# Heads finished in the projection, split float32r products and wide softmax tiles in a decoder layer

## The chip, the cores and the metric

The kernel runs on one NeuronCore of a Trainium2 chip. The metric is the device time of the whole kernel in microseconds. Engines are named as in the profile: PE is TensorE, DVE is VectorE, ACT is ScalarE, POOL is GpSimd, SP is SyncE, which issues the DMAs. Each runs its own instructions in their order, and they wait for each other through semaphores.

## The reference, cut to what matters

x holds 16 sequences of 128 tokens and 1024 features, in float32. One decoder layer: self-attention over the 128 tokens, cross-attention of a linear kind to a context of the same shape, and a gated feed-forward network with 4-bit weights (untouched by the change).

```
h = layernorm(x)
q, k, v = split(clip(h @ Wqkv.T, -8, 8))           # 1024 columns each
q = layernorm(q) * q_w + q_b;  k = layernorm(k) * k_w + k_b
scores = q @ k.T * 32**-0.5 + slope[head] * (j - i)  # 32 heads of 32, causal
x = x + softmax(scores) @ v @ Wout.T
# cross-attention: the 128 tokens are the channels, the 1024 features the positions
q2 = softmax(Wq @ layernorm(x), over the 64 of a head) * 64**-0.5   # 8 heads of 64
k2 = softmax(Wk @ ctx, over the 1024 positions);  v2 = Wv @ ctx
y = Wo @ ((k2 @ v2.T).T @ q2) + bo           # per head
x = x + y / norm(y, over 128 channels) * g * sqrt(128)
x = x + ffn(layernorm(x))
```

## The kernel before

It has three stages, one after another.

**Projection** (`qkv_phase`, L155). The 16 row tiles are normalised, transposed on PE and kept as a high and a low float32r part (`xT_hi`, `xT_lo`). The 3072 output columns come in six chunks of 512. For each chunk the weights are loaded in eight pieces through two staging slots, split by ACT (high, L231) and DVE (low, L255), and for each of the 16 tiles PE runs one product of 24 float32r matmuls: three terms (high x high, high x low, low x high) for each of eight blocks of the contraction (`product`, L309). DVE clips the result (L282), SP stores it to the tensor `qkv`.

**Attention** (`attention_phase`, L316). One turn for each of the 16 sequences, plus one. Turn b does the self-attention of sequence b ("own") and the cross-attention's query side of sequence b-1 ("cross"); it prepares sequence b+1 ("ahead"). Each engine has a function for its part of a turn (`turn_tensor` L510, `turn_scalar` L646, `turn_gpsimd` L691, `turn_vector` L730, `turn_sync` L490); the order in it is written out by hand. The body has 12 steps. In step t PE makes the scores of four heads (a tile of 128 x 512, L527), transposes the probabilities of tile t-2 (L519), multiplies tile t-3 by v (L548), makes a query tile of the cross-attention (L537), and in turns a key tile (L558), its transposes (L564), and their product with the context (L575). DVE adds the bias and takes maxima (L481, L487); ACT takes four exponentials of 128 columns with the maximum as bias and the sum as side result (L656); POOL multiplies by the reciprocal (L697).

After the steps PE multiplies for y (L604), projects by `Wout` in two halves of 24 matmuls, and between them transposes the next sequence's normalised q and k (`transpose_qk`, L421) and sums the squares of y (L626). After the second half come the context transposes (L438) and a product with a diagonal matrix that spreads 1/norm over the partitions (L643). The layer norm of q and k runs here: DVE takes statistics of `qk_in` (`qk_statistics`), POOL normalises (`normalise_qk`), ACT applies weight and bias from the transposed tiles (`norm_qk_affine`, L431) and DVE spreads k into the block-diagonal `kD` (`key_blocks`, L475). Query, key, score and norm products are float32.

**Feed-forward** (`feed_forward_phase`).

## Time and profile before

| | us |
|---|---|
| median of 3 runs | 3303.28 (3303.07 to 3303.88) |
| span of the profiled execution | 3299.9 |
| PE busy | 3128.8 |
| DVE busy | 1773.3 |
| ACT busy | 1045.8 |
| POOL busy | 507.1 |

The profile is of one execution. Its span runs from the first instruction to the last; the rest of that execution's own time is not in the records, and the median of the runs is 3.4 us above the span. Busy times are sums over an engine's instructions. Ends of matmuls are modelled: a row "x8" lasts longer than eight starts are apart, since the last one's own time is in it.

### The profile page before, as it was taken

The numbers are of one execution on the slowest core, as the hardware profiler recorded it, in microseconds if no ns is written. First come the engines' busy times: TensorE is split into PE (matmuls) and PEld (weight loads), VectorE is DVE, ScalarE is ACT, GpSimd is POOL, SyncE is SP. The second block draws the span as 40 slices with busy tenths as digits, with TensorE's granted clock in tenths as the row PEclk, the third lists the DMA queues.
The fourth block names the chain that finished last, engine by engine and source line by source line (L and its number), as shares of the span: only waits on it lengthen the run. The fifth ranks groups of instructions, "written<-read, shape, count | busy, mean of one in ns | idle before, by whom it ended". The sixth has DMA issues, their size and how long they took to land. (4 is left out here: it accounts for less than half of the span.)

```text
span 3299.9 us, 41826 instructions
## 1 busy us (share of the span) xinstructions
PE 3128.8 (95%) x15136; PEld 2393.9 (73%) x15136; DVE 1773.3 (54%) x2927; ACT 1045.8 (32%) x2356; POOL 507.1 (15%) x525
## 2 busy tenths in 40 slices
PE   7999997799999999999996799999999899999998
PEld 6888886566666666666663688888887788888887
DVE  5311112466666666666663655555555655555555
ACT  2100000566665566666651211111111211111111
POOL 2100000233333333333332100000000100000000
PEclk9999999899999999999996899999999999999999
DMA  4222223111111111111110432222122521231222
GB/s 144 93 73 75 73 70 116 41 39 38 43 46 51 38 38 39 50 38 51 38 33 31 129 82 55 76 65 75 54 82 76 153 64 54 81 81 54 62 74 78
DMA packets 83350, 218.73 MB, mean 66 GB/s; under 512 B 11984, under 2 KB 18256, under 8 KB 81232
## 3 DMA queue, kind: packets, MB, share of 16 engines
q1 hardware_dynamic: 83280, 217.78, 21.8%
q8 instruction: 46, 0.75, 0.1%
q14 instruction: 24, 0.20, 0.0%
HBM read 175.79 MB, written 41.94 MB: 66 GB/s over the span
## 5 line engine op out<-in xcount | busy, mean ns | idle before, releaser
L312 PE MATMUL ff_ps<-h_xT_hi,w_hi 128*128 128x512 f32 x1376 | 538.2, 391 | 13.2 <-DVE h_xT_lo L96 13.2
L312 PE MATMUL ff_ps<-h_xT_lo,w_hi 128*128 128x512 f32 x1376 | 537.1, 390 | 0.0
L312 PE MATMUL ff_ps<-h_xT_hi,w_lo 128*128 128x512 f32 x1376 | 537.0, 390 | 0.0
L1042 ACT ACTIVATE w_hi<-words 128x1024 fp32r<-128x1024 f32 x134 | 142.5, 1063 | 697.3 <-DVE words L1087 697.3
L1127 DVE TENSOR_TENSOR acc<-ff_po,acc 128x512 f32<-128x512 f32 x352 | 243.0, 692 | 210.6 <-PE ff_po L312 209.9
L312 PE MATMUL qkv_acc<-w_hi,xT_hi 128*128 128x512 f32 x768 | 300.9, 392 | 9.2 <-DVE w_lo L255 9.2
L312 PEld LDWEIGHTS ff_ps<-h_xT_hi,w_hi 128*128 128x128 f32 x1376 | 259.5, 189 | 68.3 <-issue 8.8
L312 PE MATMUL qkv_acc<-w_hi,xT_lo 128*128 128x512 f32 x768 | 299.4, 390 | 0.0
L312 PE MATMUL qkv_acc<-w_lo,xT_hi 128*128 128x512 f32 x768 | 299.3, 390 | 0.0
L312 PEld LDWEIGHTS ff_ps<-h_xT_hi,w_lo 128*128 128x128 f32 x1376 | 259.4, 189 | 54.1
L312 PEld LDWEIGHTS ff_ps<-h_xT_lo,w_hi 128*128 128x128 f32 x1376 | 259.6, 189 | 53.8
L312 PE MATMUL ff_po<-w_hi,h_hi 128*128 128x512 f32 x704 | 276.3, 393 | 10.1 <-DVE h_lo L1119 10.1
L282 DVE TENSOR_SCALAR qkv_out<-qkv_acc 128x512 f32<-128x512 f32 x96 | 66.4, 692 | 395.1 <-PE qkv_acc L312 395.1
L312 PE MATMUL ff_po<-w_lo,h_hi 128*128 128x512 f32 x704 | 275.8, 392 | 0.0
L312 PE MATMUL ff_po<-w_hi,h_lo 128*128 128x512 f32 x704 | 275.6, 391 | 0.0
L1115 DVE TENSOR_TENSOR gate<-gate,ff_ps 128x512 f32<-128x512 f32 (+1 forms) x88 | 60.3, 686 | 345.4 <-PE ff_ps L312 344.7
L656 ACT ACTIVATE scores<-scores,neg_max 128x128 f32<-128x128 f32 x512 | 199.2, 390 | 120.0 <-DVE neg_max L487 120.0
L231 ACT ACTIVATE w_hi<-w_stage 128x512 fp32r<-128x512 f32 x56 | 35.4, 632 | 452.8 <-DMA w_stage<-in_w_attn 452.8
L697 POOL TENSOR_TENSOR scores<-scores,row_rec 128x512 f32<-128x512 f32 x128 | 133.2, 1041 | 293.3 <-DVE row_rec L765 293.3
L312 PEld LDWEIGHTS qkv_acc<-w_hi,xT_hi 128*128 128x128 f32 x768 | 144.6, 188 | 39.1 <-DVE w_lo L255 9.6
L1087 DVE TENSOR_TENSOR words<-words,sc 128x1024 f32<-128x1024 int32 x134 | 164.2, 1226 | 4.6
L312 PEld LDWEIGHTS qkv_acc<-w_hi,xT_lo 128*128 128x128 f32 x768 | 144.4, 188 | 30.2
(156 smaller groups left out, 5305.9 us busy)
## 6 DMA issues: line engine op xcount, KB each, us to landing
words<-in_w SPq DMA_DIRECT2D x90, 512.0 KB, 3.5
qkv<-qkv_out SPq DMA_DIRECT2D x96, 256.0 KB, 2.0
words<-in_w SPq DMA_DIRECT2D x176, 128.0 KB, 4.0
sc<-in_s SPq DMA_DIRECT2D x88, 256.0 KB, 4.3
qk_in<-qkv SPq DMA_DIRECT2D x16, 1024.0 KB, 4.9
w_stage<-in_w_attn SPq DMA_DIRECT2D x56, 256.0 KB, 3.0
qkv_rows<-in_x SPq DMA_DIRECT2D x16, 512.0 KB, 3.8
ctx_in<-in_context SPq DMA_DIRECT2D x16, 512.0 KB, 3.7
```

What stands on the lines that cost most here:

```text
L231: nc.scalar.activation(dst[:, r, :], stage[:, r % 2, :], ACT.Copy).then_inc(w_hi_done, 1)
L282: nc.vector.tensor_scalar(res[:, :], acc[:, t % BANKS, :], CLIP, -CLIP, ALU.min, ALU.max).then_inc(clipped, 1)
L312: last = nc.tensor.matmul(out, left, right, start=n == 0, stop=n == len(pairs) - 1)
L656: last = nc.scalar.activation(sc[:, t % SR, j, :], sc[:, t % SR, j, :], ACT.Exp, bias=neg_max[:, t, j:j + 1], accum_out=row_sum[:, t, j:j ...
L697: nc.gpsimd.tensor_tensor(sc[:, n % SR, :, :], sc[:, n % SR, :, :], row_rec[:, n, :].unsqueeze(2).to_broadcast([P, HG, P]), ALU.mult).then ...
L1042: nc.scalar.activation(dst, src, ACT.Copy).then_inc(s["split_hi"], 1)
L1087: nc.vector.tensor_tensor(dst, src, scale, ALU.mult).then_inc(s["scaled"], 1)
L1115: nc.vector.tensor_tensor(gate[sl][0:units, :], gate[sl][0:units, :], b, ALU.mult).then_inc(s["product"], 1)
L1127: nc.vector.tensor_tensor(cols, po[:, o % 4, :], cols, ALU.add).then_inc(s["added"], 1)
```

## The change

In the projection (now `projection_phase`) the row tiles are taken in two halves of eight, so there are 12 rounds (two halves of six chunks), all written out without a loop. Clipped q and k stay on chip until both chunks of a row tile are there; then DVE has their statistics, POOL normalises, PE transposes and ACT applies weight and bias; SP stores them transposed as `qh` and `kh`. v is clipped and stored as before, through two slots. The first weights go to a buffer of their own. Rows 8 to 15 are loaded and normalised in the sixth round (`ci == 5`).

In attention, q comes as it is used, and k is loaded straight into the diagonal blocks of `kD` by four DMAs. The query and key products of the cross-attention become three-term float32r products (`wqk_hi`, `wqk_lo`, `xn_hi`, `xn_lo`, `ctx_hi`, `ctx_lo`). Score tiles 1, 3, 5 and 7 are "wide": POOL subtracts the maxima, ACT takes one exponential of 512 columns, DVE sums. The body has 10 steps: what steps 0 and 1 did (scores 0 and 1, key tile 0, the first transposes) now stands at the end of the turn before (`second_lead`, `lead_scalar`). 1/norm is spread by eight transposes of a broadcast column. kT holds two tiles; y has a tile of its own.

```diff
+    TILES = NB // 2
+    ROUNDS = 2 * QKV_CHUNKS
...
+    def follows(ci, t, tiles):
+
+        was = ci * TILES + t - tiles
+        if was < 0 or was // TILES % QKV_CHUNKS not in (1, 3):
+            return None
+        return heads_before(was // TILES, was % TILES)
...
+            for r in range(0, KT, 2):
+                if r == 2:
+                    load_rows(1)
+                sp.dma_start(left[:, r:r + 2, :], w_attn[0, :, r:r + 2, :]).then_inc(w_first[r // 2], 16)
...
+            for ci in range(ROUNDS):
+                half, chunk = half_and_chunk(ci)
+                for t in range(TILES):
+                    load(ci + 1, t)
+                    if ci == 0 and t + 3 < TILES:
                         load_rows(t + 3)
-                    if t % 2 == 0:
-                        load(c + 1, t // 2)
-                    sp.wait_ge(clipped, c * NB + t + 1 + BANKS)
-                    sp.dma_start(qkv[t, :, bass.ds(c * N, N)], res[:, :]).then_inc(stored, 16)
-
-            chunks(sp, chunk)
-            sp.wait_ge(stored, 16 * (QKV_CHUNKS * NB + 1))
+                    if ci == 4 and t < 2:
+                        load_rows(TILES + t)
+                    if (m := follows(ci, t, 2)) is not None:
+                        store_heads(m)
+                    if chunk >= 4:
+                        n = values_before(ci, t)
+                        sp.wait_ge(s["clipped"], ci * TILES + t + 1)
+                        sp.dma_start(v[half * TILES + t, :, (chunk - 4) * N:(chunk - 3) * N],
+                                     res[:, n % 2, :]).then_inc(v_stored[n % 2], 16)
+                    if ci == 5 and t + 2 < TILES:
+                        load_rows(TILES + t + 2)
...
+            def normalise_heads(m):
+                t, p = m % TILES, m % 2
+                pool.wait_ge(s["h_mom"], m + 1)
+                nc.gpsimd.tensor_tensor(h_mom[:, p, 4:5], h_mom[:, p, 3:4], half_neg[:, :], ALU.pow).then_inc(
+                    s["h_rstd"], 1)
+                pool.wait_ge(s["h_rstd"], m + 1)
+                for part in (left[:, t, :], right[:, p, :]):
+                    last = nc.gpsimd.tensor_scalar(part, part, h_mom[:, p, 2:3], h_mom[:, p, 4:5], ALU.add, ALU.mult)
+                last.then_inc(s["h_normed"], 1)
...
+            def scale_heads(m):
+                kind = m // TILES % 2
+                if m == 0:
+                    act.wait_ge(s["affine_in"], 4 * 16)
+                act.wait_ge(s["h_turned"], m + 1)
+                if m >= 2:
+                    act.wait_ge(h_stored[m % 2], m // 2 * 16)
+                for k in range(KT):
+                    last = nc.scalar.activation(heads[:, m % 2, k, :], room[m % 2][:, k, :], ACT.Identity,
+                                                scale=affine[:, 2 * kind, k:k + 1],
+                                                bias=affine[:, 2 * kind + 1, k:k + 1])
+                last.then_inc(s["h_out"], 1)
...
+                nc.vector.tensor_scalar(dst, acc[:, at % 4, :], CLIP, -CLIP, ALU.min, ALU.max).then_inc(
+                    s["clipped"], 1)
+                if chunk < 4:
+                    dve.wait_ge(s["clipped"], at + 1)
+                    first = chunk % 2 * 6
+                    nc.vector.bn_stats(h_stats[:, t, first:first + 6], dst).then_inc(s["h_stats"], 1)
...
+                    if ci == 5:
+                        if t == 0:
+                            statistics(TILES)
+                        if t + 1 < TILES:
+                            statistics(TILES + t + 1)
...
+                    low(ci + 1, t, w_hi[1 - ci % 2], w_lo[1 - ci % 2])
+                    clip(ci, t)
+                    if ci % QKV_CHUNKS in (1, 3):
+                        head_moments(ci, t)
+                    if ci == 5:
+                        ln.low(dve, TILES + t, t, room[t % 2])
...
+            def turn_heads(m):
+                pe.wait_ge(s["h_normed"], m + 1)
+                if m >= 2:
+                    pe.wait_ge(s["h_out"], m - 1)
+                for k in range(KT):
+                    part_of = (left[:, m % TILES, :], right[:, m % 2, :])[k // 4]
+                    last = nc.tensor.transpose(room[m % 2][:, k, :], part_of[:, k % 4 * P:(k % 4 + 1) * P], ident[:, :])
+                last.then_inc(s["h_turned"], 1)
...
+                    part(ci, t)
+                    if (m := follows(ci, t, 1)) is not None:
+                        turn_heads(m)
+                    if ci == 5:
+                        if t == 0:
+                            pe.wait_ge(s["h_out"], 2 * TILES)
+                        ln.transpose(pe, TILES + t, t % 2, room[t % 2])
...
+    WIDE = (1, 3, 5, 7)
...
+    def load_heads(sp, b):
+        sp.dma_start(hT[:, :, :], qh[b, :, :].rearrange("p (a d) -> p a d", a=KT)).then_inc(s["q_loaded"], 16)
+        for j in range(HG):
+            at = slice(j * HD, (j + 1) * HD)
+            sp.dma_start(kD[at, :, j, :], kh[b, at, :].rearrange("p (a d) -> p a d", a=KT)).then_inc(s["kd_loaded"], 16)
...
+    def keys(pe, b, i):
+        for e in range(2):
+            at = slice(e * N, (e + 1) * N)
+            last = product(nc, pair_k[:, at], [(w[:, 1, i * P:(i + 1) * P], c[:, at]) for w, c in (
+                (wqk_hi, ctx_hi), (wqk_hi, ctx_lo), (wqk_lo, ctx_hi))])
+        last.then_inc(s["k_done"], 1)
...
+    def exponentials(act, b, t):
+        if t in WIDE:
+            act.wait_ge(s["s_subbed"], wide_count(b, t))
+            last = nc.scalar.activation(sc[:, t % SR, :, :], sc[:, t % SR, :, :], ACT.Exp)
+        else:
+            act.wait_ge(s["s_max"], b * G + t + 1)
+            for j in range(HG):
+                last = nc.scalar.activation(sc[:, t % SR, j, :], sc[:, t % SR, j, :], ACT.Exp,
+                                            bias=neg_max[:, t, j:j + 1], accum_out=row_sum[:, t, j:j + 1])
+        last.then_inc(s["s_exp"], 1)
...
+    def keys_out(act, b, i):
+        act.wait_ge(s["kt_done"], b * XT + i + 1)
+        if i >= 2:
+            act.wait_ge(s["m_done"], b * XT + i - 1)
+        nc.scalar.activation(flat(kT[:, i % 2, :, :]), pair_k[:, :], ACT.Copy).then_inc(s["kt_out"], 1)
...
+    def rows_high(act, c, e):
+        act.wait_ge(s["x1_norm"], 2 * c + e + 1)
+        at = slice(e * N, (e + 1) * N)
+        nc.scalar.activation(xn_hi[:, at], xn[:, at], ACT.Copy).then_inc(s["xn_hi_done"], 1)
+
+    def rows_low(dve, c, e):
+        dve.wait_ge(s["xn_hi_done"], 2 * c + e + 1)
+        at = slice(e * N, (e + 1) * N)
+        nc.vector.tensor_tensor(xn_lo[:, at], xn[:, at], xn_hi[:, at].bitcast(F32), ALU.subtract).then_inc(
...
+    def subtract_maxima(pool, b, t):
+        pool.wait_ge(s["s_max"], b * G + t + 1)
+        nc.gpsimd.tensor_tensor(sc[:, t % SR, :, :], sc[:, t % SR, :, :],
+                                neg_max[:, t, :].unsqueeze(2).to_broadcast([P, HG, P]), ALU.add).then_inc(
+            s["s_subbed"], 1)
+
+    def reciprocals(dve, b, t):
+        dve.wait_ge(s["s_exp"], b * G + t + 1)
+        if t in WIDE:
+            nc.vector.tensor_reduce(row_sum[:, t, :], sc[:, t % SR, :, :], AX.X, ALU.add).then_inc(s["s_summed"], 1)
+            dve.wait_ge(s["s_summed"], wide_count(b, t))
+        nc.vector.reciprocal(row_rec[:, t, :], row_sum[:, t, :]).then_inc(s["s_rec"], 1)
...
+        if ahead:
+            sp.wait_ge(s["ctx_lo_done"], b + 1)
+            sp.wait_ge(s["c_done"], b + 1)
+            sp.dma_start(ctx_in[:, :], ctx_kv[b + 1, :, :]).then_inc(s["ctx_loaded"], 16)
...
+            sp.wait_ge(s["s_done"], (b + 1) * G)
+            load_heads(sp, b + 1)
             sp.wait_ge(s["o_done"], b + 1)
+            sp.dma_start(v_in[:, :], v[b + 1, :, :]).then_inc(s["v_loaded"], 16)
...
+                at = slice(j * P, (j + 1) * P)
+                product(nc, bank_q[:, :], [(r[:, at], w[:, 0, :]) for r, w in (
+                    (xn_hi, wqk_hi), (xn_hi, wqk_lo), (xn_lo, wqk_hi))]).then_inc(s["q_done"], 1)
...
+            scores(pe, b + 1, 0)
...
+            pe.wait_ge(s["ctx_lo_done"], b + 2)
+            keys(pe, b + 1, 0)
...
+            for k in range(KT):
+                last = nc.tensor.transpose(norm_banks[k // 4][:, k % 4, :],
+                                           n_sq[:, 1, k:k + 1].to_broadcast([P, P]), ident[:, :])
...
+    def second_lead(pe, b):
+        pe.wait_ge(s["s_biased"], b * G + 1)
+        scores(pe, b, 1)
+        turn_probabilities(pe, b, 0)
+        turn_keys(pe, b, 0)
+        pe.wait_ge(s["kt_out"], b * XT + 1)
+        transpose_context(pe, b)
...
+    def lead_scalar(act, b, follows=True):
+        exponentials(act, b, 0)
+        key_exponentials(act, b, 0)
+        exponentials(act, b, 1)
+        probabilities_out(act, b, 0)
+        keys_out(act, b, 0)
+        if follows:
+            rows_high(act, b - 1, 0)
+        context_out(act, b)
+        if follows:
+            rows_high(act, b - 1, 1)
...
+        for j in range(STEPS):
+            n = j + 1
+            if own and n < G:
+                normalise_scores(pool, b, n)
+            if own and j + 2 in WIDE:
+                subtract_maxima(pool, b, j + 2)
...
+        if ahead:
+            subtract_maxima(pool, b + 1, 1)
...
+            if own and j + 2 < G:
+                bias_scores(dve, b, j + 2)
+            if own and j + 1 in WIDE[1:]:
+                reciprocals(dve, b, j + 1)
...
+                context_low(dve, b + 1)
...
+        if ahead:
+            bias_scores(dve, b + 1, 0)
+            maxima(dve, b + 1, 0)
...
+            reciprocals(dve, b + 1, 0)
...
+        if ahead:
+            key_maxima(dve, b + 1, 0)
...
+            bias_scores(dve, b + 1, 1)
+            maxima(dve, b + 1, 1)
+        if own:
+            rows_low(dve, b, 0)
+        if ahead:
+            reciprocals(dve, b + 1, 1)
+        if own:
+            rows_low(dve, b, 1)
```

## Rows read from the trace of the kernel before

**Rows 1.** The page, parts 1: span; busy time (share of the span) and instructions of the TensorE.

```profile
span 3299.9 us, 41826 instructions
...
PE 3128.8 (95%) x15136; PEld 2393.9 (73%) x15136; DVE 1773.3 (54%) x2927; ACT 1045.8 (32%) x2356; POOL 507.1 (15%) x525
```

**Rows 2.** Instructions on `qkv_acc`: count, ns min/median/max, first and last start.

```profile
L312 PE MATMUL qkv_acc<-w_hi,xT_hi x768: 389/389/796, 24.1 to 559.9; 128*128 128x512 f32 x192
```

**Rows 3.** PE timeline, turns 0 and 1: start, us, line, tiles, count, [idle before].

```profile
636.64 0.50 PE L312 MATMUL pair_o<-w_hi,oT_hi 128*128 128x512 f32 x1
...
664.99 1.02 PE L537 MATMUL bank_q<-wqk_sb,xn 128*128 128x512 f32 x2
...
673.50 1.02 PE L527 MATMUL bank_s<-kD,qkT 128*128 128x512 f32 x2
...
684.12 1.02 PE L527 MATMUL bank_s<-kD,qkT 128*128 128x512 f32 x2
...
705.11 3.60 PE L604 MATMUL bank_s<-qT,z 128*128 128x512 f32 x8
```

**Rows 4.** PE timeline, the last two turns of attention.

```profile
1725.57 3.60 PE L604 MATMUL bank_s<-qT,z 128*128 128x512 f32 x8
...
1759.10 2.07 PE L537 MATMUL bank_q<-wqk_sb,xn 128*128 128x512 f32 x2 [0.66 <-DVE qr L752]
```

**Rows 5.** PE timeline, one steady turn.

```profile
1012.27 0.40 PE L312 MATMUL pair_o<-w_lo,oT_hi 128*128 128x512 f32 x1
...
1017.64 1.03 PE L438 MATMUL pair_k<-ident,ctx_in 128*128 128x128 f32 x8
1018.52 1.02 PE L643 MATMUL bank_q<-xn,ones 128*128 128x512 f32 x2
...
1021.09 1.88 PE L558 MATMUL pair_k<-ctx_in,wqk_sb 128*128 128x512 f32 x4
...
1025.94 1.09 PE L564 MATMUL pair_k<-ident,kE 128*128 128x128 f32 x8 [2.11 <-ACT kE L673]
...
1027.37 1.92 PE L527 MATMUL bank_s<-kD,qkT 128*128 128x512 f32 x2
```

**Rows 6.** One stretch of attention: us; busy (x count) of PE, PEld, DVE, ACT, POOL; PEclk; DMA.

```profile
1001.00:1075.00 74.00, 70.99 (x397) 46.65 (x396) 48.69 (x100) 45.44 (x122) 27.24 (x28) 0.98 0.14 43
```

**Rows 7.** All engines in order of time, the start of the kernel.

```profile
11.65 1.20 POOL L79 TENSOR_SCALAR qkv_rows<-qkv_rows,ln_moments 128x1024 f32<-128x1024 f32 x1
12.27 1.11 DVE L255 TENSOR_TENSOR w_lo<-w_stage,w_hi 128x512 fp32r<-128x512 f32 x1 [1.13 <-ACT w_hi L231]
...
24.07 0.80 PE L312 MATMUL qkv_acc<-w_hi,xT_hi 128*128 128x512 f32 x1 [9.20 <-DVE w_lo L255]
```

**Rows 8.** The page, part 6: DMA issues, count, KB each, us to landing.

```profile
w_stage<-in_w_attn SPq DMA_DIRECT2D x56, 256.0 KB, 3.0
qkv_rows<-in_x SPq DMA_DIRECT2D x16, 512.0 KB, 3.8
```

**Rows 9.** DVE timeline of the steady turn.

```profile
1019.77 0.14 DVE L816 TENSOR_SCALAR x_mom<-x_mom 128x1 f32<-128x1 f32 x1
...
1053.12 1.23 DVE L758 TENSOR_REDUCE kneg<-pair_k 128x1 f32<-128x1024 f32 x1 [0.39 <-PE pair_k L558]
...
1054.92 0.68 DVE L481 SCALAR_TENSOR_TENSOR scores<-bank_s,alibi 128x512 f32<-128x512 f32 x1
...
1056.95 0.69 DVE L752 TENSOR_TENSOR qr<-bank_q,q_max 128x512 f32<-128x512 f32 x1
```

**Rows 10.** ACT timeline of the steady turn.

```profile
1024.70 1.09 ACT L673 ACTIVATE kE<-pair_k,kneg 128x1024 f32<-128x1024 f32 x1
...
1042.37 0.61 ACT L662 ACTIVATE qr<-qr 128x512 f32<-128x512 f32 x1
```

**Rows 11.** POOL timeline of the steady turn.

```profile
1038.53 1.04 POOL L697 TENSOR_TENSOR scores<-scores,row_rec 128x512 f32<-128x512 f32 x1 [2.18 <-DVE row_rec L765]
```

**Rows 12.** All engines, the start of attention: the first biased scores.

```profile
591.52 0.69 DVE L481 SCALAR_TENSOR_TENSOR scores<-bank_s,alibi 128x512 f32<-128x512 f32 x1 [2.34 <-PE bank_s L527]
```

More of the change, by code:

```diff
@@ L265, in _ @@
             statistics(1)
[L266 removed]
+            for r in range(1, KT // 2):
                 low(0, r, w_hi[0], w_lo[0])
[L268 to L269 removed]
+            ln.low(dve, 0, 0, room[0])
+            for r in range(KT // 2, KT):
                 low(0, r, w_hi[0], w_lo[0])
[L272 to L274 removed]
+            for ci in range(ROUNDS):
+                for t in range(TILES):
+                    if ci == 0 and t + 2 < TILES:
@@ L664, in turn_scalar @@
+        for j in range(STEPS):
+            if own and 0 < j < G:
+                probabilities_out(act, b, j)
+            if own and j + 2 < G:
+                exponentials(act, b, j + 2)
+            if cross and j < KT:
+                act.wait_ge(s["q_subbed"], c * KT + j + 1)
+                nc.scalar.activation(qr[:, j % SR, :], qr[:, j % SR, :], ACT.Exp).then_inc(s["q_exped"], 1)
+            n = j - 2
             if cross and 0 <= n < KT:
```

674 lines of the change are left out of this document (331 added, 343 removed).

## The prediction

> **What bounds the kernel now.** I read the page's head first: the reader is to see a span of 3299.9 us and a TensorE that is busy for 95% of it [rows 1]. The span lies 3.4 us under the median of the runs, 3303.3. All sums below are differences, so they are added to the median. The kernel has three stages: the projection, whose matmuls run from 24.1 to about 560.7 [rows 2]; attention, to about 1810; the feed-forward network, which the change leaves alone. The chain of waits names only the last stage, so for the first two I used the timelines of PE, DVE, ACT and POOL.
>
> Projection: 2304 matmuls fill 24.1 to 560.7 with 128 transposes between them. The stage is PE's, and whatever is added to PE there is paid in full.
>
> Attention: I measure a turn from one cross-attention product y to the next. The first begins at 705.11 and the fifteenth at 1725.57 [rows 3, 4], so 14 turns take 72.9 us each. PE stands almost back to back. It waits once for more than 1 us, 2.11 us for the first key exponential, and behind that wait the scores product can take 1.92 instead of 1.02 us, at half clock [rows 5]. In a stretch of 74 us PE is busy for 71.0, DVE for 48.7, ACT for 45.4 and POOL for 27.2 [rows 6]. DVE is second, and it stands in chains with ACT and POOL, so I also asked what these chains permit once PE has less to do.
>
> **Part 1, the projection.** *Head transposes.* q and k are now turned here: 32 pairs of tiles x 8 = 256 transposes. Eight take 0.88 us from 1017.64 to 1018.52 [rows 5], so 32 x 0.88 = +28.2 us, all on PE. They follow the product by one tile (5.44 us), and the chain behind it fits: clip 0.7, statistics 0.7, aggregation 0.5, power and two half-row scalings on POOL about 2.3, together 4.2 us with the latencies.
>
> *Start.* The eight weight pieces no longer share two staging slots, and a product starts with its first low piece. Before, PE began at 24.07, waiting for the last low piece [rows 7]. Now it should begin when the first turned row has its low part, about 14 to 15: -9.5 us (bounds: 0 if the DMAs land no sooner, -11).
>
> *Sixth round.* Here rows 8 to 15 are normalised while v is clipped. One loop closes over SP, which issues the next row only after waiting for the clip: store issue 0.4, row landing 3.8 [rows 8], two statistics and moments 1.7, low weight 0.6, clip 0.7, latencies 0.1: 7.3 us a tile, against PE's 5.44 + 0.88 = 6.32. Over seven tiles DVE falls 6.5 us behind, and the next round waits for its last low weight: +5.9. After such an idle stretch PE starts at half clock, which costs another 1.7 (2 x (1.92 - 1.02) us, as behind the wait in [rows 5]): +7.6. In the other value rounds the loop load-split-clip-store (0.4 + 3.0 [rows 8] + 0.7 + 0.7 + 0.7) just equals 5.44, with 0.4 us late at each round's end, three times: +1.2. Bounds for both: 0, if four accumulator banks absorb it, to 14.
>
> Sum: +28.2 - 9.5 + 8.8 = +27.5.
>
> **Part 2, a steady attention turn.** *PE work removed.* The 16 transposes of q and k: -1.75. Three-term products: the pitch in a float32r product is (1017.64 - 1012.27)/23 = 0.233 us, three are 0.70; a float32 product is two passes of 0.43 (four take 1.88, two 1.02, so 0.43 for one more) [rows 5], 0.86. Sixteen such products a turn: 16 x 0.16 = -2.6. The norm: four passes of 0.43 become eight transposes: -0.85. Together -5.2 us a turn. If PE stayed the bound this would be 73 us over 14 turns. I don't think it does, for two reasons.
>
> *The lead (what is late next, first).* Let y start at 0. PE: y 6.9, projection half 5.6, scores(0) 0.9, norm sums 1.8, second half, ends 20.7; keys(0) to 22.1, norm transposes 23.0, scores(1) 23.8, transposes of probabilities 0 24.3. DVE ends the moments of x1 2.2 us behind the second half (1019.91 against 1017.64) [rows 5, 9], so 22.9; key maximum 1.2 [rows 9]: 24.1; ACT's exponential with what follows takes 1.24 until PE starts (1024.70 to 1025.94) [rows 5, 10]: PE waits from 24.3 to 25.4 and turns the keys to 26.3. DVE meanwhile scales y by two banks (25.3), adds the bias of scores 1 (25.9), takes its maxima (26.6). POOL subtracts them, 1.04 [rows 11]: 27.7; the one exponential of 512 columns 0.63 [rows 10]: 28.4. **ACT is in order**: behind that exponential stand the copy of the probabilities (0.5) and the copy of the turned keys (1.0), done at 29.9, though the keys lay ready at 26.4. PE's context transposes wait for it: idle from 26.3 to 29.9. Then ACT splits a half of xn, copies the context and splits the other half (32.5), and DVE, which has the low half, the sum of scores 1 and the low half in its order, reaches bias(2) at 33.15. So the lead has 4.7 us of PE idle, where the 2.1 us stood. q(0) starts at 31.6, against 72.2 - 40.1 = 32.1 before (664.99 to 705.11 is 40.1 [rows 3]; 72.2 is what PE's parts and waits of a turn add up to where no half clock follows the wait, 73.9 where it does).
>
> *The steps (second).* DVE's even step now carries the sum of the wide tile beside the key maximum. From bias to the start of the key maximum it was 2.03 + 0.60 (1054.92 to 1056.95 [rows 9], and one pitch); sum and reciprocal add 0.84. So: scores start +1.06 bias, +3.47 key maximum, +1.22 its end, 0.25 until ACT is free, +1.24: PE can turn keys 7.24 us after the scores, and needs only 6.3 for its own work. The rest of the pair (0.93 + 1.79 + 0.87 of PE) makes 10.84 us for two steps, where PE took 684.12 - 673.50 = 10.62 [rows 3]. The PE time saved becomes waits. The same count through ten steps puts the next y at 73.0: 9.8 + 10.84 + 20.7 behind q(0) at 31.6. With the late bias(2) the steps take 41.4 instead of 40.1.
>
> *Clock.* PE does few products between 24 and 31, and I expect the half clock behind it in every turn, not in some. As DVE is the bound there until about 37, I charge 0.2 (0 to 0.9).
>
> *A port.* POOL's scaling at 11.65 and DVE's subtraction of two SBUF tiles at 12.27 stood together, and the latter took 1.11 us instead of 0.69 [rows 7]. The new low half at 32.5 stands beside POOL's normalisation and is on the chain: +0.4 (0 to 0.5). The wide maxima have no such partner.
>
> The Trainium skill, GPSIMD Engine Reference, section Key points, says that GpSimd shares its SBUF interfaces with VectorE and contends with instructions that have two SBUF inputs; the trace agrees with that pair of rows. By the rule the 0.4 us is paid in every turn, as I take it; without it the sum would be 14 x 0.4 = 5.6 us less.
>
> Turn after: 73.0 + 0.2 + 0.4 = 73.6 against 72.9: +0.7, over 14 turns +9.8. Bounds: 71.5 (the waits overlap better than I laid out by hand) to 75.
>
> **Part 3, the ends of attention.** Start: the first bias stood at 591.52 [rows 12] behind statistics, transposes, affine and key blocks. Now memset before the first loads (+3.6), weights split ahead of it on DVE: bias near 587, and scores(2) near 597 instead of 602: -5. Turn 0's own steps: 9.15 against 9.0 us a pair, nothing. Between its projection at 636.64 and q(0) at 664.99 lay 28.35 us [rows 3] with the q/k load and statistics in it; now 5.6 + 0.9 + 5.6 + the lead's 10.9 without y = about 23: -5.4, and +1.3 for the late bias(2) in the following steps. End: eight q steps alone at half clock (2.07 us for a pair of passes [rows 4]) save 0.4 each on their chain, but q(0) waits for two splits more: -1.7. Together -10.8 (bounds -20 to -3). SP's new order (context first, five head loads after the last scores, v before the store) leaves each load over 15 us; nothing. If that cover went, a 3.8 us landing would show.
>
> **Sum:** 27.5 + 9.8 - 10.8 = +26.5 us: 3303.3 + 26.5 = **3330 us**.
>
> **Rivals.**
> - *A, PE stays the bound* (faster). ACT and DVE clear their queues inside PE's work, the lead's idle stays at 2 us and the steps keep 5.2 us less: 14 x -5.2 = -73, with 27.5 and -10.8: 3247. For it: PE is busy for 71.0 of 74 us and DVE for 48.7 [rows 6]. Against it: the order on ACT (exponential 1 ahead of both copies) is fixed. A half-way case, turns of 71 us: 14 x -1.9 + 16.7 = -10, 3293. It decides from 71.7 us a turn down.
> - *B, the projection is cheap:* no loop in the sixth round, full gain at the start: -9 from my sum; with 73.0 a turn another -8: 3312.
> - *C, the clock* (slower still). The half clock after the lead lasts past the first steps, where PE is short of time again; one more scores and q pair at half clock is 0.9 + 0.8, so about 1.5 us more a turn: 3351. For it: the wait of 2.11 us is followed by the half clock [rows 5], and the new waits are longer. Against it: from 34 us on PE has products again.
>
> The Trainium skill, TensorE: Matmul & The Clock Gate, section Part 4, says transposes don't count as busy for the clock; the lead has 20 of them around its waits, so by that rule C is likelier. The trace shows the half clock starting just after transposes [rows 5], in agreement.
>
> **Chances.** Forecast with its neighbourhood 3315 to 3345: 0.45; B 0.17; C 0.11; A with its half-way case 0.27. A change under 0.2% (6.6 us) is about what a measurement of this kernel can't tell from none. Faster 0.25 (most of A), same 0.09 (the rest of A, the low edge of B), slower 0.66. Range 3275 to 3350, down to a little beyond A's half-way case and up to C; the likeliest case's own is 3315 to 3345.
>
> **What would show it.** Head transposes 28 us and projection end near 588; a stretch of idle PE before the seventh round; turns of 73.6 us between y products; PE waiting 3 to 4 us for the copy of turned keys; waits for the key exponential near 0.9 us in odd steps. I am wrong if turns fall under 72, or if attention's DVE shows idle time ahead of bias(2).

## The result and the profile after

The changed kernel takes 3336.05 us (median of 4 runs, 3335.66 to 3336.91) against 3303.18 for the kernel before (4 runs): 1.010 times as long, interval 1.0088 to 1.0112, +32.9 us. The forecast was 3330, with a range from 3275 to 3350.

The page's head of the changed kernel answers to [rows 1]: TensorE has lost 26 us of work and the span has grown by 33.8 us.

```profile
span 3333.7 us, 42083 instructions
...
PE 3103.1 (93%) x15456; PEld 2460.2 (74%) x15456; DVE 1819.4 (55%) x3024; ACT 1035.4 (31%) x2005; POOL 585.4 (18%) x621
```

**Projection.** The matmuls of the projection by tile, as in [rows 2]: they start at 14.7 instead of 24.1 (-9.4) and end 30.4 us later. From its first matmul to its last (14.67 to 590.77, where it was 24.07 to 560.31) the stage has grown by 39.9 us.

```profile
L397 PE MATMUL qkv_acc<-w_hi,xT_hi x768: 389/389/792, 14.7 to 590.3; 128*128 128x512 f32 x192
```

All engines in the sixth round of the projection (start, us, engine, line, tiles, idle before it):

```profile
298.14 0.69 DVE L345 TENSOR_SCALAR v_out<-qkv_acc 128x512 f32<-128x512 f32 x1
298.86 0.34 SPq L246 DMA_DIRECT2D v<-v_out  x1
299.25 0.43 SPq L216 DMA_DIRECT2D qkv_rows<-in_x  x1
...
303.01 0.69 DVE L63 BATCH_NORM_STATS2 ln_stats<-qkv_rows 128x6 f32<-128x512 f32 x1 [3.04 <-DMA qkv_rows<-in_x]
...
305.30 0.68 DVE L345 TENSOR_SCALAR v_out<-qkv_acc 128x512 f32<-128x512 f32 x1
...
311.08 0.79 PE L397 MATMUL qkv_acc<-w_hi,xT_hi 128*128 128x512 f32 x1 [2.84 <-DVE w_lo L321]
...
319.69 0.69 DVE L345 TENSOR_SCALAR head_left<-qkv_acc 128x512 f32<-128x512 f32 x1 [2.92 <-PE qkv_acc L397]
```

Read them as a circle: clip 298.14, store, next rows issued at 299.25, statistics at 303.01, next clip 305.30. A tile takes 7.16 us (six tiles of this round take 7.1 to 7.5). At the end PE waits 2.84 us for the last low weight and then runs at half clock (1.2 instead of 2.4 GHz): the first product of the next round takes 8.41 us instead of 5.44, and its clip comes 8.75 us after the one before (310.94).

**A steady turn of attention.** PE, as in [rows 5], from one y product of the cross-attention to the next:

```profile
1025.98 3.60 PE L757 MATMUL bank_s<-qT,z 128*128 128x512 f32 x8
...
1051.05 1.09 PE L559 MATMUL pair_k<-ident,kE 128*128 128x128 f32 x8 [0.81 <-ACT kE L584]
1055.52 1.97 PE L564 MATMUL pair_k<-ident,ctx_in 128*128 128x128 f32 x8 [3.37 <-ACT kT L591]
1057.28 1.92 PE L540 MATMUL bank_s<-kD,hT 128*128 128x512 f32 x2
...
1072.38 1.02 PE L540 MATMUL bank_s<-kD,hT 128*128 128x512 f32 x2
...
1075.04 1.09 PE L559 MATMUL pair_k<-ident,kE 128*128 128x128 f32 x8 [0.59 <-ACT kE L584]
...
1083.00 1.02 PE L540 MATMUL bank_s<-kD,hT 128*128 128x512 f32 x2
...
1099.65 3.60 PE L757 MATMUL bank_s<-qT,z 128*128 128x512 f32 x8
```

From the first y (731.67) to the fifteenth (1761.21) a turn takes 73.54 us; it was 72.89. Ten of the fourteen turns take 73.7 us; in the two shortest (73.05) the context transposes run at nearly full clock (1.18 and 1.13 us instead of 1.97). The wait of 2.11 us [rows 5] has become 0.81 + 3.37 us, and 0.59 us of waiting stands in each later pair of steps (10.62 us from one scores product to the next but one: as before [rows 3], though with less PE work in it).

ACT in the same lead (the end of a turn, where the first steps of the next sequence are done) shows what the 3.37 us are: exponential 1 waits 2.43 us for GpSimd, and the copy for which PE waits (1054.45) stands behind it.

```profile
1049.79 1.11 ACT L584 ACTIVATE kE<-pair_k,kneg 128x1024 f32<-128x1024 f32 x1 [6.75 <-DVE kneg L647]
...
1053.43 0.63 ACT L574 ACTIVATE scores<-scores 128x512 f32<-128x512 f32 x1 [2.43 <-POOL scores L634]
1053.97 0.58 ACT L569 ACTIVATE probT<-bank_p 128x512 f32<-128x512 f32 x1
1054.45 1.02 ACT L591 ACTIVATE kT<-pair_k 128x1024 f32<-128x1024 f32 x1
```

One turn as a stretch, as in [rows 6] (there 74 us): PE is busy for 67.1 of 73.6 us, at a granted clock of 0.95.

```profile
1030.50:1104.10 73.60, 67.14 (x401) 49.28 (x400) 45.66 (x91) 37.27 (x81) 27.90 (x28) 0.95 0.14 43
```

**Start of attention**, all engines: the fill of the key blocks comes first, four key loads take 2.64 us to issue, and ACT, DVE and PE all wait for the last small load, issued at 606.21, behind eleven others. VectorE's bias for scores 0 then stands behind the low halves of the weights (until 620.9).

```profile
596.22 3.51 POOL L1043 MEMSET kD<- 128x4096 f32 x1 [91.00 <-POOLq L205]
...
600.14 2.64 SPq L537 DMA_DIRECT2D kD<-kh  x4
...
606.21 0.45 SPq L1032 DMA_DIRECT2D g_sb<-in_g  x1
...
612.26 1.06 ACT L1060 ACTIVATE wqk_hi<-kE 128x1024 fp32r<-128x1024 f32 x1 [19.96 <-DMA g_sb<-in_g]
...
620.86 0.68 DVE L620 SCALAR_TENSOR_TENSOR scores<-bank_s,alibi 128x512 f32<-128x512 f32 x1
```

**Where the 33.8 us of the span lie:** start of the projection -9.4, its length +39.9, from its last matmul to the first y 144.8 to 140.9 = -3.9, fourteen turns +9.1, the last turn +0.9, from the last y to the end -2.8 (the norm's transposes in place of the diagonal product).

### The profile page after: what moved, and what is told of

The parts are those of the page before. It is cut to its first block and busy times, and to the rows that moved or that the text cites. A ratio compares the mean times of both kernels' runs of the same rounds, so it can differ in the third digit from the quotient of the medians.

```text
span 3333.7 us, 42083 instructions
## 1 busy us (share of the span) xinstructions
PE 3103.1 (93%) x15456; PEld 2460.2 (74%) x15456; DVE 1819.4 (55%) x3024; ACT 1035.4 (31%) x2005; POOL 585.4 (18%) x621
## 5 line engine op out<-in xcount | busy, mean ns | idle before, releaser
L76 POOL TENSOR_TENSOR ln_moments<-ln_moments,half_neg 128x1 f32<-128x1 f32 x32 | 21.4, 670 | 861.3 <-DVE ln_moments L69 844.2
L321 DVE TENSOR_TENSOR w_lo<-w_stage,w_hi 128x512 fp32r<-128x512 f32 x96 | 70.6, 736 | 180.6 <-ACT w_hi L284 180.6
L540 PE MATMUL bank_s<-kD,hT 128*128 128x512 f32 x256 | 146.1, 655 | 23.9 <-DMA g_sb<-in_g 21.1
```

Source lines behind the costliest of these rows:

```text
L76: nc.gpsimd.tensor_tensor(self.moments[:, p, 4:5], self.moments[:, p, 3:4], self.half_neg[:, :], ALU.pow).then_inc(self.rstd_done, 1)
L321: nc.vector.tensor_tensor(lo[:, r, :], src, hi[:, r, :].bitcast(F32), ALU.subtract).then_inc(s["w_lo_done"], 1)
L540: nc.tensor.matmul(bank_s[:, :], hT[:, t, :], flat(kD[:, t, :, :]), start=True, stop=True).then_inc(s["s_done"], 1)
```

## The experiments

All were run beside the kernel before. Where a difference to the changed kernel is given, it is one of medians. The projection's last matmul stood between 588.6 and 591.6 in the profiles of seven kernels with the same projection, so differences of up to 3 us there say nothing.

**1. Rows loaded ahead of the clip.**

```diff
+                    if ci == 5 and t + 2 < TILES:
+                        load_rows(TILES + t + 2)
                     if chunk >= 4:
                         n = values_before(ci, t)
...
-                    if ci == 5 and t + 2 < TILES:
-                        load_rows(TILES + t + 2)
```

> The changed kernel with one edit: in the sixth round of the projection SP issues the load of the next rows of x ahead of its wait for the clip of v, not behind it. Theory (the sixth round is a loop clip - row load - statistics - clip, 7.3 us a tile against 6.35 of PE work, and the seventh round then waits for its last low weight and runs at half clock): the loop opens, clips of the sixth round stand 6.4 us apart, the 2.84 us wait goes, and the time falls by 6 to 8 us, to about 3329 (25.5 us over the kernel before). Rival (the round is held by the weight path, load - split - low half, which this edit does not touch): clips stay 7.2 us apart and the time stays within 1 us of 3336.

Measured 3329.25 us (1.0077, 1.006 to 1.0094): -6.8. The clips of the sixth round, VectorE:

```profile
286.84 0.68 DVE L345 TENSOR_SCALAR v_out<-qkv_acc 128x512 f32<-128x512 f32 x1
293.58 0.69 DVE L345 TENSOR_SCALAR v_out<-qkv_acc 128x512 f32<-128x512 f32 x1
299.61 0.69 DVE L345 TENSOR_SCALAR v_out<-qkv_acc 128x512 f32<-128x512 f32 x1
305.35 0.68 DVE L345 TENSOR_SCALAR v_out<-qkv_acc 128x512 f32<-128x512 f32 x1
311.26 0.69 DVE L345 TENSOR_SCALAR head_left<-qkv_acc 128x512 f32<-128x512 f32 x1
```

The spacings shown lie between 5.7 and 6.7 us (the round's first is 7.6, the others 6.2 to 6.4), the next round follows without a gap, and the last matmul of the projection starts at 582.5, 8.3 us earlier. The loop was the one named.

**2. ACT's copies ahead of exponential 1.**

```diff
         key_exponentials(act, b, 0)
-        exponentials(act, b, 1)
         probabilities_out(act, b, 0)
         keys_out(act, b, 0)
+        exponentials(act, b, 1)
```

> The changed kernel with one edit: in the lead of each attention turn ACT copies probabilities 0 and turned keys 0 to SBUF ahead of the exponential of wide tile 1, not behind it. Theory (ACT is in order, and the wait for GpSimd's subtraction stands in front of the copy for which PE waits 3.4 us): PE's wait for the keys falls to about 1.2 us, a turn from 73.5 to about 72, and the time by 15 to 30 us over 15 leads, to about 3314. Rival (the lead is held by the DVE chain that ends in bias 2, the PE wait only moves): the turn stays within 0.3 us and the time within 4 us of 3336.

Measured 3307.48 us (1.0014, 1.0005 to 1.0024): -28.6, nearly the whole loss, from the order of two lines. PE in the lead:

```profile
1042.02 1.09 PE L559 MATMUL pair_k<-ident,kE 128*128 128x128 f32 x8 [0.81 <-ACT kE L584]
1044.23 1.09 PE L564 MATMUL pair_k<-ident,ctx_in 128*128 128x128 f32 x8 [1.11 <-ACT kT L591]
1045.15 1.02 PE L540 MATMUL bank_s<-kD,hT 128*128 128x512 f32 x2
```

3.37 us of waiting became 1.11, and in thirteen of the fourteen turns what follows runs at full clock (1.09 and 1.02 us instead of 1.97 and 1.92). A turn takes 71.50 us (730.95 to 1732.00 over 14).

**3. All tiles narrow** (the wide softmax undone).

```diff
-    WIDE = (1, 3, 5, 7)
+    WIDE = ()
```

and the two calls that subtract the maxima of tile 1 dropped.

> The changed kernel with the wide softmax undone: all eight score tiles of a turn go back to four exponentials with ACT's own bias and sum, no subtraction on GpSimd, no sum on VectorE. Theory (the wide tiles put 0.84 us of VectorE work ahead of the key maximum in every even step and a wait for GpSimd in front of ACT's copies in the lead): waits for the key exponential in odd steps vanish, the wait for the turned keys falls to 2 us or less, a turn to 71.5 to 72 us, the time by 20 to 30 us, to about 3311. Rival (the wide tiles relieve ACT of 2 us a pair of steps, and ACT would be what PE waits for): the turn grows by 0.5 us or more and the time passes 3343. A second rival, that TensorE alone sets the turn: within 4 us of 3336.

Measured 3307.96 us (1.0014, 1.0005 to 1.0024): -28.1. PE, one lead and one pair of steps:

```profile
1046.60 1.97 PE L564 MATMUL pair_k<-ident,ctx_in 128*128 128x128 f32 x8 [3.25 <-ACT kT L591]
1048.36 1.92 PE L540 MATMUL bank_s<-kD,hT 128*128 128x512 f32 x2
...
1063.46 1.02 PE L540 MATMUL bank_s<-kD,hT 128*128 128x512 f32 x2
...
1065.46 1.09 PE L559 MATMUL pair_k<-ident,kE 128*128 128x128 f32 x8
...
1073.42 1.02 PE L540 MATMUL bank_s<-kD,hT 128*128 128x512 f32 x2
```

The expectation had two effects, and only one came. The pair falls from 10.62 to 9.96 us and its wait is gone. The lead's wait stays at 3.25 us: exponential 1 stands ahead of the copy in either form. A turn takes 71.74 us.

**4. One term for q and keys.**

```diff
-    (xn_hi, wqk_hi), (xn_hi, wqk_lo), (xn_lo, wqk_hi)
+    (xn_hi, wqk_hi),
```

and likewise for the key products.

> The changed kernel with the q and key projections of attention cut from three float32r products to the first one (the products with the low halves are left out; the low halves are still made and waited for). It takes 16 x 2 x 0.233 = 7.5 us of TensorE work out of a turn. Theory of the prediction (the new turn is held by the chains through ACT and DVE, saved TensorE work turns into waits): TensorE's waits in a turn grow by 5 us or more, the turn falls by 0 to 2 us, the time by 5 to 30 us, to no less than 3306. Rival (TensorE still sets the turn, with only 6.4 us of waits in 73.5): the turn falls by 5 us or more, 16 turns by 80 to 115 us, to about 3240.

Measured 3343.04 us (1.0115, 1.0098 to 1.0132): 7.0 us *slower* than with three terms, outside both expectations. PE, in one of the longer turns:

```profile
1064.72 1.92 PE L559 MATMUL pair_k<-ident,kE 128*128 128x128 f32 x8 [1.51 <-ACT kE L584]
1066.43 2.81 PE L727 MATMUL pair_o<-kT,ctxT 128*128 128x128 f32 x16
...
1073.81 1.02 PE L540 MATMUL bank_s<-kD,hT 128*128 128x512 f32 x2
1084.42 1.02 PE L540 MATMUL bank_s<-kD,hT 128*128 128x512 f32 x2
```

Two things are to be seen. The pair of steps (1073.81 to 1084.42) still takes 10.61 us, although 1.8 us of PE work has been taken from it: it is not PE's. And in the turn shown half clock reaches the first steps: the turning of the keys takes 1.92 instead of 1.09 us and the next product 2.81 instead of 1.95, on a stretch where their end counts. That happens in eight of the fourteen turns, which take 74.8 us; the other six take 73.2, about 0.5 less than most turns of the changed kernel. The mean is 74.11 us. So 7.5 us less TensorE work bought at most 0.5 us a turn, and more than that was lost where the half clock fell on the steps.

**5. One of eight head blocks turned.**

```diff
-                for k in range(KT):
+                for k in range(1):
                     part_of = (left[:, m % TILES, :], right[:, m % 2, :])[k // 4]
```

and ACT scales the one turned block eight times.

> The changed kernel with seven of the eight transposes of each q or k head tile left out of the projection (ACT scales the one turned block eight times; 32 x 7 = 224 transposes are not done). Theory (the projection is TensorE's, every transpose there is paid in full): 224 x 0.11 = 24.7 us, less what the stalls of the sixth round keep, so the last projection matmul comes at 565 to 568 instead of 591 and the time falls by 23 to 26 us, to about 3311. Rival (the chain clip - statistics - GpSimd scaling - turn, or ACT's eight scalings, holds the rounds with heads): clips stay over 6 us apart there and the time falls by under 15 us.

Measured 3311.64 us (1.0027, 1.0014 to 1.004): -24.4, against 24.7 by count. A round whose heads are turned and the round behind it take 88.2 us together instead of 94.3; there are four such pairs, so 24.2 us. There the head transposes are paid in full. The last projection matmul comes at 568.2, 22.5 us earlier, since the sixth round has grown longer (57.7 instead of 55.9 us).

**6. q as one two-pass product.**

```diff
-                product(nc, bank_q[:, :], [(r[:, at], w[:, 0, :]) for r, w in (
-                    (xn_hi, wqk_hi), (xn_hi, wqk_lo), (xn_lo, wqk_hi))])
+                product(nc, bank_q[:, :], [(xn[:, at], wqk_hi[:, 0, :].bitcast(F32))])
```

and `rows_high`, `rows_low` dropped.

> The changed kernel with the q projection of attention back to one float32 product of the normalised rows (with the high half of the weights; their low half is left out), so that ACT and VectorE no longer split the rows in the lead; the key projection keeps three terms. Theory (the pairs of steps are held by the chain scores - bias - key maximum - key exponential, 10.62 us, with 0.6 us of TensorE slack, and in the lead the splits stand on the chain): TensorE's 0.16 us more for each of 8 products is hidden, pairs stay at 10.6 us, q(0) and the bias of scores 2 come 0.5 to 1.5 us earlier: a turn falls by 0.3 to 1 us, the time by 5 to 15 us, to about 3327. Rival (three terms pay, TensorE's time counts): a turn grows by 1.3 us, the time by about 18 us, to 3354. The 0.4 us that the prediction charged for the port is not expected as a gain of its own: the low half stood at 0.69 us.

Measured 3329.80 us (1.0081, 1.0064 to 1.0098): -6.3. In the profile a turn takes 73.38 us (-0.16, 2.3 us over fourteen), the last one 56.15 instead of 57.30, and the projection ended 1.3 us earlier, which the edit doesn't touch. The total lies in the range, but the gain of a turn is smaller than the 0.3 to 1 us expected. TensorE's longer products cost the turn nothing in sum, and leaving out the splits gained little.

**7. Attention's loads ahead of the fill.**

```diff
-            sp.wait_ge(s["filled"], 1)
-            load_heads(sp, 0)
+            sp.dma_start(hT[:, :, :], qh[0, :, :].rearrange("p (a d) -> p a d", a=KT)).then_inc(s["q_loaded"], 16)
             sp.dma_start(ctx_in[:, :], ctx_kv[0, :, :]).then_inc(s["ctx_loaded"], 16)
...
             sp.dma_start(g_sb[:, :], g.rearrange("a p b -> p (a b)")).then_inc(s["setup_in"], 16)
+            sp.wait_ge(s["filled"], 1)
+            for j in range(HG):
+                at = slice(j * HD, (j + 1) * HD)
+                sp.dma_start(kD[at, :, j, :], kh[0, at, :].rearrange("p (a d) -> p a d", a=KT)).then_inc(
+                    s["kd_loaded"], 16)
             sp.dma_start(x1[:, :], x[0, :, :]).then_inc(s["x_loaded"], 16)
```

> The changed kernel with one edit at the start of attention: SP issues the loads that don't write the key blocks (q, context, weights, v, gains) at once, and waits for the 3.5 us fill of the key blocks only ahead of the four key loads. Theory (the start of attention is a chain fill 3.5 - nine load issues - last small load - splits - first bias, which is why the expected 5 us did not come): the setup loads are complete near 606 to 608 instead of 612.3, the first bias comes 4 us earlier, and the time falls by 3 to 5 us, to about 3332. Rival (the first bias waits for the alibi mask made on VectorE and GpSimd, or for the landing of the weight pieces at the DMAs' rate): within 1.5 us of 3336.

Measured 3330.73 us (1.0085, 1.0068 to 1.0102): -5.3. The last small load releases the engines at 604.80 instead of 612.26, but the first bias comes at 616.08 instead of 620.86: VectorE now waits 2.8 us for the weight pieces of the projection by `Wout`, whose low halves stand ahead of the bias. The projection of this profile ended 2.1 us earlier too; from its last matmul to the first y it is 137.4 instead of 140.9 us, so 3.5 us belong to the edit.

**8. Edits 1, 2, 3 and 7 together.**

> The changed kernel with four edits together: next rows loaded ahead of the wait for the clip in the sixth round, ACT's copies ahead of exponential 1 in the lead, all tiles narrow, and the loads of attention issued ahead of the wait for the fill. Measured alone the first three gave -6.8, -28.6 and -28.1 us. Theory (the second takes the lead's wait and its half clock, the third the chain of the pairs: different places, so they add): a turn of 69.5 to 70 us, the time near 3336 - 67 = 3269, 1% under the kernel before. Rival (the second and the third remove the same wait of the lead, or TensorE alone sets the turn once one is gone): a turn of 71 us or more and 3290 to 3300.

Measured 3290.65 us (0.9963, 0.9951 to 0.9974): 45.4 us under the changed kernel, where the four alone add up to 68.8. A turn takes 71.14 us on average, but of two kinds: 70.1 (996.83 to 1066.95) and 71.7 (1066.95 to 1138.70). PE in a turn of the second kind, and VectorE in one of the first:

```profile
1103.78 1.77 PE L559 MATMUL pair_k<-ident,kE 128*128 128x128 f32 x8 [1.05 <-ACT kE L584]
```

```profile
1027.58 1.02 DVE L605 TENSOR_TENSOR xn_lo<-xn,xn_hi 128x512 fp32r<-128x512 f32 x1 [0.65 <-ACT xn_hi L600]
1028.52 0.68 DVE L620 SCALAR_TENSOR_TENSOR scores<-bank_s,alibi 128x512 f32<-128x512 f32 x1
```

Scores 2 are done at 1026.1 here (1025.04 and 1.02 us), and their bias starts at 1028.52, behind the low half of rows that q(4) reads first. The scores that come next are late too, PE waits 1.05 us for the key exponential behind them in every turn, and in nine of the fourteen turns half clock follows that wait. Added up, experiments 2 and 3 would give a turn of 69.7 us. The shorter turns take 70.1, 0.4 us more; in nine turns the half clock adds 1.6 us each, 14.6 of the 20 us that are missing in the fourteen. What VectorE's order holds back beyond that shows only in experiment 9.

**9. That low half moved to step 1, and ACT's rounding of the first half moved ahead of its copies.** Against experiment 8:

```diff
          key_exponentials(act, b, 0)
+        if follows:
+            rows_high(act, b - 1, 0)
         probabilities_out(act, b, 0)
         keys_out(act, b, 0)
         exponentials(act, b, 1)
-        if follows:
-            rows_high(act, b - 1, 0)
         context_out(act, b)
...
+            if cross and j == 1:
+                rows_low(dve, c, 1)
...
-        if own:
-            rows_low(dve, b, 1)
```

> The kernel with the four edits and a fifth: in the lead ACT rounds the first half of the normalised rows right behind the key exponential, copies the context last but one, and VectorE makes the low half of the second half in step 1 of the turn (q(4) is the first to read it), no longer ahead of the bias of scores 2. Theory (behind the lead the turn is still held by VectorE's queue: q(0) waits 0.83 us for its low half, bias 2 stands 2.3 us behind the end of scores 2, and the late bias makes the waits of 0.76 and 1.05 us that follow): these waits fall by 1.5 us or more together, the turn from 70.1 us (71.7 us where a half clock falls into it) to 68.5 to 69.5, the time by 10 to 30 us from 3290, to about 3272. Rival (TensorE is the bound of the turn by now, 65.7 us of it busy, and waits only move): turn and time within 4 us of 3290. Rival two (the half clock comes in more turns since TensorE's work is spread otherwise): slower than 3294.

Measured 3243.05 us (0.9819, 0.9805 to 0.9832): 47.6 us under experiment 8, more than the theory gave, and the best version: 60 us under the kernel before. A turn takes 68.18 us (714.00 to 1668.56 over 14), ten of 67.7 and four of 69.1 to 69.4. So the shorter turns became 2.4 us shorter still, and four turns instead of nine have the half clock on their path. The two moves were not run apart. PE, lead of one turn:

```profile
1081.38 1.09 PE L564 MATMUL pair_k<-ident,ctx_in 128*128 128x128 f32 x8 [1.11 <-ACT kT L591]
1082.32 1.02 PE L540 MATMUL bank_s<-kD,hT 128*128 128x512 f32 x2
...
1085.75 1.02 PE L540 MATMUL bank_s<-kD,hT 128*128 128x512 f32 x2
```

Scores 3 follow scores 2 by 3.4 us; in experiment 8 it was 4.5 (1025.04 to 1029.51).

**10. The wait of 3.4 us filled.**

```diff
         turn_keys(pe, b, 0)
+        if follows:
+            pe.wait_ge(s["x1_done"], 2 * b)
+            product(nc, pair_o[:, 0:N], [(oT_hi[:, k % KT, :], w_hi[1][:, k % KT, :]) for k in range(12)])
         pe.wait_ge(s["kt_out"], b * XT + 1)
```

> The changed kernel with 12 products of 512 columns put on TensorE in the lead of each turn behind the transposes of the turned keys, where it waits 3.4 us for ACT's copy (12 x 0.23 = 2.8 us, nobody reads them). Theory (the half clock behind the lead, scores 2 in 1.92 us instead of 1.02 and its neighbours, comes from the 3.4 us in which TensorE does nothing): scores 2 takes 1.02 us, the context transposes 1.09, and a turn falls by 0.9 to 1.7 us although it has more work; the time falls by 10 to 25 us, to about 3320. Rival (the half clock comes from the transposes or costs nothing because VectorE is the bound there): the turn stays within 0.3 us and the time within 4 us of 3336, or grows by what the filling delays.

Measured 3336.83 us (1.0105, 1.0089 to 1.012): +0.8, nothing in sum. PE, in one of the longer turns:

```profile
1053.96 1.09 PE L564 MATMUL pair_k<-ident,ctx_in 128*128 128x128 f32 x8 [0.60 <-ACT kT L591]
1054.88 1.02 PE L540 MATMUL bank_s<-kD,hT 128*128 128x512 f32 x2
...
1062.69 1.61 PE L559 MATMUL pair_k<-ident,kE 128*128 128x128 f32 x8 [1.05 <-ACT kE L584]
```

The first half of the theory holds: without the idle time the context transposes and scores 2 run at full clock. The second holds in nine turns, for less than expected: the bias of scores 2 comes 33.1 instead of 33.7 us after y, and these turns take 73.05 us, 0.6 less than most turns of the changed kernel. In the other five half clock appears in step 1, behind the next wait (1.05 us), and they take 74.7 us. The mean is 73.64 us. So the half clock behind the lead cost 0.6 us a turn, and one step later it costs 1.6, since there the end of PE's work counts.

**11 and 12. The best version with two parts of the change exchanged:** q in two passes as in experiment 6, and the wide tiles kept (`WIDE = (1, 3, 5, 7)`).

> The kernel with the five edits (3243 us), with the q projection back to one float32 product of two passes (with the high half of the weights; their low half is left out) and no splits of the rows in the lead. Alone on the changed kernel this edit gave -6 us. Theory (with narrow tiles and the lead in order, TensorE sets the pairs of steps, 9.96 us without a wait, so its time counts again): 8 x 0.16 = 1.3 us more a turn, less 0 to 0.4 us of splits in the lead, 15 turns: +13 to +20, about 3259. Rival (the VectorE and ACT work of the splits is worth more than TensorE's passes here too): 3240 or less.

Measured 3251.02 us (0.9844, 0.9827 to 0.986): +8.0, less than the 13 to 20 expected, but with the theory's sign. A pair takes 10.3 instead of 9.96 us (1025.42 to 1035.73), and 0.32 was to be expected. Turns at full clock take 68.6 instead of 67.7, +0.84: of the 1.3 us of longer products the lead gives back 0.44, about what was allowed. The rest of the miss lies in the last turn (56.15 instead of 57.29 us) and in the half clock, which lengthens two turns instead of four.

> The kernel with the five edits (3243 us), but with the wide tiles of the change kept: four of eight tiles with one exponential, the subtraction on GpSimd and the sum on VectorE. Theory (the wide tiles are a loss by themselves: their 0.84 us on VectorE stand ahead of the key maximum in every even step and hold a pair at 10.6 us where TensorE needs 9.96): pairs of 10.6 us, waits of 0.6 us for the key exponential, a turn of 70 instead of 68.2 us, the time 24 to 30 us above 3243, about 3270. Rival (wide tiles cost only where the lead was in the wrong order): within 6 us of 3243.

Measured 3272.85 us (0.9906, 0.9889 to 0.9922): +29.8, a turn 69.97 us, with the waits of 0.59 us back in the later odd steps. The wide tiles are a loss in either order of the lead (28.1 us with the old one, 29.8 with the new).

## Why the prediction was right

The change cost 32.9 us where 26.5 were forecast, and the time is inside the range. In the span the projection gave +30.5 us for 27.5, the fourteen turns +9.1 for 9.8, and the ends of attention -5.8 for -10.8.

*The bound.* Right: the turn is not PE's. Experiment 4 took PE work away and lost time; experiment 2 added none and removed none, only reordered ACT, and gained 28.6 us.

*Head transposes, +28.2.* Right: a tile with its head transposes takes 6.35 us where one without takes 5.44, 29.0 us for the 32, and leaving out 224 of 256 gave 24.2 us in these rounds (experiment 5).

*Start, -9.5.* Right: -9.4 (first matmul at 14.67 instead of 24.07 [rows 7]).

*Sixth round, +7.6.* Right in place, mechanism and near in size: 7.16 us a tile for 7.3, and opening the loop gave 6.8 us. Its parts were otherwise: the half clock behind it cost 3.0 us (8.41 instead of 5.44 for one product) for the 1.7 predicted, the round's own delay was about 5.1 for 5.9 (seven tiles at 7.3 instead of 6.32 us would even make 6.9). The stage grew by 39.9 where these terms and +1.2 for the other rounds make 37.0. The trace shows where the 2.9 us are, within 0.3: 0.8 in the head transposes, 0.5 here, and 1.9 in the other rounds of v, for which 0.4 us of lateness three times was predicted: the fifth round ends 1.9 us late (1.71 of them PE's wait for the last low weight) and the eleventh 1.2.

*Steady turn, +0.7 a turn.* Measured +0.65. The parts: PE waits 3.37 us for the copy of the turned keys where 3.6 was predicted, 0.59 us in later odd steps where I expected 0.9, a pair at 10.62 where I had 10.84, the bias of scores 2 33.7 us behind y where I had 33.15 plus the charges. The charge of 0.4 us for the port was not due: the low half took 0.69 us at 1059.10, because GpSimd had ended its scaling just before. Instead the half clock cost all of the 0.6 us that I had given to clock and port: with full clock in the lead (experiment 10) turns take 73.05 us and the bias of scores 2 stands at 33.1, where I had 73.0 and 33.15. Where the pair of engines did overlap it cost 0.33 us (experiment 8). In experiment 10 it took 0.96 us, so 0.27 of its 33.1 are the port's. So the port was charged too high, the clock too low, and that the two errors cancel in the sum is luck.

*Ends of attention, -10.8.* The term that was mis-sized: -5.8 measured. The start, -9.1 by my steps, was -3.9. The step that was off is "bias near 587, and scores(2) near 597": I counted the fill, but not that SP issues the q load, four key loads and six others behind it, ahead of the last small load that releases ACT, DVE and PE at 612.26. Scores 2 came 40.5 us behind the projection instead of 41.2, 0.7 us sooner where I had 5. Experiment 7 gave 3.5 us of it back.

The end came to -1.9 us for -1.7 by luck. The last turn, which I had at -1.7, took 0.9 us longer: its eight q steps save 0.43 us each (3.15 instead of 3.58), as I said, but q(0) comes 27.1 us behind y instead of 23.7. Of these 3.4 us, 2.2 are one instruction: VectorE's low half for which q(0) waits stands beside GpSimd's sum and takes 2.91 us instead of 0.69. The charge for the port was due here, and larger than the one I made in the steady turn. What hid it is the tail, in no term of mine: there the norm's eight transposes replace four passes, and the end comes 2.8 us sooner.

*Rivals.* A (PE stays the bound) fell with experiment 4, and its half-way case (turns of 71 us) is what experiment 2 reached (71.5) once ACT's order was another. Its grounds, PE busy for 71 of 74 us, were sound numbers read for the wrong question: they say what PE does now, not what stands behind it. B fell with experiment 1. C, the clock: the half clock came behind the lead's wait in twelve of fourteen turns, but it ended before the steps where PE is short of time and cost 0.6 us, not the 1.5 us more that C asks for. In experiment 4, with still less PE work, it reached these steps in eight of fourteen turns, as C describes (74.8 us).

The Trainium skill, TensorE: Matmul & The Clock Gate, Part 4, says that transposes don't count as busy in the same way. Experiments 2 and 10 keep every transpose of the lead, one with less waiting before the context transposes (1.11 instead of 3.37 us), one with products in place of it, and both run them at full clock. So the transposes alone did not bring the half clock; what share they have in it the runs don't show.

## What to carry to other kernels

On an engine that works in order, put what another engine waits for ahead of what itself waits: one exponential that waited for GpSimd held back a copy that was ready, 2 us a turn. When the bounding engine's work shrinks, write down the chain that stands next with its own durations before claiming the gain; here the chain through VectorE took 10.6 us a pair of steps, just what TensorE had taken. And take a combination's gain from its own run: four edits gave 45 of 69 us, and a fifth, a new order of the row splits on ACT and VectorE, gave 48.

## What the runs showed of the hardware

- Less TensorE work made the kernel slower (experiment 4, +7.0 us): with 7.5 us less of products a turn, half clock reaches steps where it counts in eight of fourteen turns (74.8 us against 73.2).
- Turns of one kernel come in two lengths, mostly 1.4 to 1.65 us apart (70.1 and 71.7 in experiment 8; 67.7 and 69.3 in experiment 9; 73.05 and 74.7 in experiment 10; in the kernel before 72.3 and 73.9). In experiments 8 and 10 half clock meets the turning of the keys or the product behind it in the longer ones and not in the shorter, though PE waits 1.05 us ahead of them in both; in experiment 9 it meets the context transposes, behind a wait of 1.11 us. Ten runs of experiment 8 spread from 3277.7 to 3298.2 us.
- VectorE's subtraction of two SBUF tiles took 0.69 us alone and 1.02 beside GpSimd's product of scores and reciprocals (512 columns); beside GpSimd's sum of two 1024-column tiles one took 1.83 us (experiment 9, where it cost nothing) and two took 3.52 us in the last turn of the changed kernel, the first alone 2.91. The Trainium skill, GPSIMD Engine Reference, Key points, names this contention; what it costs depends on the order of both queues, and a single row does not tell whether it will be met. VectorE at the last turn, beside GpSimd:

```profile
1785.35 3.52 DVE L605 TENSOR_TENSOR xn_lo<-xn,xn_hi 128x512 fp32r<-128x512 f32 x2 [1.15 <-ACT xn_hi L600]
1785.37 2.35 POOL L910 TENSOR_TENSOR res<-y,res 128x1024 f32<-128x1024 f32 x1
```
